# Two-layer attention and expert kernel: queries and keys turned by DMA, GpSimd's split ahead of its value step, and a third PSUM bank for the first score pass

## What is computed

```
q = (x @ Wq.T + bq).reshape(B, L, H, hd); k, v likewise
q = _apply_rope(q, cos, sin); k = _apply_rope(k, cos, sin)      # layer 0
scores = jnp.einsum('bqhd,bkhd->bhqk', q, k) / np.sqrt(hd)
attn = jax.nn.softmax(scores, axis=-1)
out = jnp.einsum('bhqk,bkhd->bqhd', attn, v).reshape(B, L, D)
x = _layernorm(x + out @ Wo.T + bo)
```

## Time and profile before

| | us |
|---|---|
| median of 3 runs | 602.04 (600.29 to 603.62) |
| profiled execution | 603.38, its span 601.6 |
| attention of layer 0, first scores to last maxima | about 17 to 126 |
| attention of layer 1 | about 252 to 367 |
| ScalarE, VectorE busy in the span | 413.9, 429.6 |

### The profile page before, as it was taken

How to read it: one execution, slowest core, us unless ns; L and a number is a source line. 1 busy time by engine, 2 the same in 40 slices (tenths; PEclk the granted TensorE clock), 3 DMA queues, 4 the chain that set the end, 5 groups by cost and what they waited for, 6 DMA issues and landing times.

```text
span 601.6 us, 16720 instructions
## 1 busy us (share of the span) xinstructions
PE 538.7 (90%) x5262; PEld 388.6 (65%) x5262; DVE 429.6 (71%) x1582; ACT 413.9 (69%) x1104; POOL 344.2 (57%) x471
## 2 busy tenths in 40 slices
PE   9899999999779984799999999979999999999950
PEld 7444444447557973544555444758889999999940
DVE  4979999966765304877989996786887788643276
ACT  2279998882624752538999988417778888999824
POOL 4978888342005782673445544456566777777730
PEclk9979999998999997958999999779999999999975
DMA  7493000002001237007910000112221122111363
GB/s 215 112 322 101 2 1 3 2 2 71 7 1 43 47 40 223 6 1 218 302 46 2 3 2 1 54 39 58 51 52 54 59 62 61 59 58 55 125 186 120
DMA packets 53204, 43.12 MB, mean 72 GB/s; under 512 B 14992, under 2 KB 43424, under 8 KB 52992
## 3 DMA queue, kind: packets, MB, share of 16 engines
q1 hardware_dynamic: 45568, 29.98, 17.3%
q0 software_dynamic: 7264, 11.62, 7.4%
q10 hardware_dynamic: 288, 0.46, 0.2%
HBM read 30.17 MB, written 11.87 MB: 70 GB/s over the span
## 4 chain that ended last, share of the span: by engine, by line
PE 70%; DVE 12%; issue 6%; DMA 5%; ACT 4%; POOL 2%; DVEq 0%; ACTq 0%; POOLq 0%; SPq 0%
PE bank L1329 12%; PE bank L1339 11%; PE bank L928 10%; PE bank L911 7%; PE bank L893 6%; PE bank L945 3%; ACT prob L1477 2%; DMA parts<-augs,idx_s 2%; PE bank L969 2%; DVE W L1965 2%; PE bank L1141 2%; PE bank L1382 1%; PE bank L1161 1%; PE bank L953 1%; PE bank L1200 1%
## 5 line engine op out<-in xcount | busy, mean ns | idle before, releaser
L1792 DVE TENSOR_REDUCE mx<-bank 128x2 f32<-128x512 f32 x256 | 163.1, 686 | 24.7 <-PE bank L893 23.7
L1477 ACT ACTIVATE prob<-bank 128x512 f32<-128x512 f32 x256 | 140.7, 609 | 23.0 <-PE bank L911 19.1
L1666 ACT ACTIVATE queries<-bank,prob 128x128 f32<-128x128 f32 x316 | 90.4, 369 | 19.9 <-PE bank L1329 17.0
L1329 PE MATMUL bank<-keys,prob 128*128 x632 | 85.7, 278 | 0.8 <-issue 0.6
L1339 PE MATMUL bank<-W,queries 128*128 x632 | 84.2, 276 | 0.0
L804 POOL DMA_INDIRECT prob<-xs,idx_g x64 | 61.8, 966 | 33.7 <-DVE idx_g L2176 12.6
L1329 PEld LDWEIGHTS bank<-keys,prob 128*128 128x128 f32 x632 | 76.8, 192 | 3.9 <-issue 2.6
L893 PE MATMUL bank<-keys,queries 32*128 32x256 f16 x512 | 77.0, 285 | 2.6 <-issue 1.7
L1339 PEld LDWEIGHTS bank<-W,queries 128*128 128x128 f32 x632 | 76.7, 192 | 1.8 <-issue 0.7
L928 PE MATMUL bank<-prob,augs 128*32 128x256 f32 x1024 | 77.7, 392 | 0.0
L813 POOL DMA_INDIRECT parts<-augs,idx_s x64 | 63.4, 991 | 21.5 <-issue 9.0
(11 more groups left out here) (292 smaller groups left out, 1045.3 us busy)
## 6 DMA issues: line engine op xcount, KB each, us to landing
W<-in_w SPq DMA_DIRECT2D x48, 256.0 KB, 4.0
sum<-zero SPq DMA_DIRECT2D x3, 1024.0 KB, 9.1
xs<-X SPq DMA_DIRECT2D x2, 768.0 KB, 5.2
prob<-xs,idx_g POOLq DMA_INDIRECT x80, 2.6
XB<-sum SPq DMA_DIRECT2D x1, 1024.0 KB, 4.9
Y<-sum SPq DMA_DIRECT2D x4, 256.0 KB, 5.7
W<-sum SPq DMA_DIRECT2D x4, 256.0 KB, 6.5
parts<-augs,idx_s POOLq DMA_INDIRECT x64, 2.2
```

The source lines that it names most:

```text
L1329: last = nc.tensor.matmul(bank[2 + p % 2][:, P * f:P * f + P], wc[:, p % 4, P * f:P * f + P], xsT2[:, bass.ds(at, 1), :], start=True, stop ...
L1477: nc.scalar.activation(prob[:, v % 8, :, :], st_bank(b, v)[:, :], ACT.Exp, scale=SCALE).then_inc(exp_done, 1)
L1666: last = nc.scalar.activation(hid2[:, p % 4, f, :], bank[2 + p % 2][:, P * f:P * f + P], ACT.Gelu, bias=wc[:, p % 4, WB + f:WB + f + 1])
L1792: nc.vector.tensor_reduce(m_at, bank[S1B[u % 2]][:, :].rearrange("p (j k) -> p j k", j=2), AX.X, ALU.max).then_inc(s1_used, 1)
```

## The change

- **Turning.** For batches 1 to 7 of each layer SyncE turns `aug` by two transposing DMAs (`turn`), one for each half t of 128 tokens, each moving queries and keys at once. They write `qkT`, which has three buffers and lies where `keys` does. TensorE's `query_transposes` and `key_transposes`, VectorE's `q_evac` and ScalarE's `keys_evac` remain for batch 0 of each layer alone. The first product of a batch waits for `turned_in`.
- **A signal for each half.** `aug_ready` is raised after each half of the split; all waits on it count twice.
- **GpSimd's order.** `build_aug` of batch i + 1 comes before `build_vaug` of batch i.
- **Third bank.** Bank 6, which took the turned keys, joins `S1B`. A unit of the first pass waits for the maxima three units back, not two.
- **SyncE's order.** The constants come after batch 1's turn. The expert weights come in groups behind turns: in layer 0 four after batch 2's and four after batch 3's, the zeroing after batch 4's; in layer 1 three after each, from batch 2 on.
- `max_transposes` now waits for the evacuation of batch i + 1's projection, which uses bank M5 too.
- `front_evac` keeps its wait for `vaug_ready`.

```diff
-        S1B, STB, OTB, M5, M6, M7 = (0, 1), (2, 3), 4, 5, 6, 7
+        S1B, STB, OTB, M5, M6, M7 = (0, 1, 6), (2, 3), 4, 5, 6, 7
...
+            def turn(lay, b):
+
+                g = b + NB * lay
+                if b > 2:
+                    sp.wait_ge(st_done, 16 * (g - 2))
+                wait_for(sp, turned_in, 32 * (g - 1 - lay))
+                for t in range(2):
+                    sp.wait_ge(aug_ready, 2 * g + t + 1)
+                    sp.dma_start_transpose(qkT[b % 3][:, t, :, :], aug[b % 2][:, t, :, :].rearrange("p h x -> p (h x)")
+                                           ).then_inc(turned_in, 16)
+
+            def batches_in(lay):
+
+                at = ((0, 0, 4, 8, 8, 8, 8, 8), (0, 0, 3, 6, 9, 12, 15, 16))[lay]
+                for b in range(1, NB):
+                    turn(lay, b)
...
             def pool_iteration(lay, i, par):
 
-                build_vaug(lay, i, par)
                 if i < NB - 1:
                     build_aug(pool, lay, i + 1, 1 - par)
+                build_vaug(lay, i, par)
...
+                if i > 0 and u == 0:
+                    pe.wait_ge(turned_in, 32 * (g - lay))
...
+                if g > 0 or u > 2:
+                    pe.wait_ge(s1_used, 16 * g + u - 2)
...
-                    if u == 13 and front_on:
-                        query_transposes(lay, i + 1, nxt)
...
-                    if u == 15 and front_on:
-                        key_transposes(lay, i + 1, nxt)
```

More of the change, by code:

```diff
@@ L145, in program @@
         queries = sb("queries", [P, 4 * NF * P])
-        QT = [queries[:, 512 * i:512 * i + 512].bitcast(F16).rearrange("p (j l) -> p j l", j=NJ) for i in range(2)]
         keys = sb("keys", [P, RING * P])
-        keyT = [keys[:, 512 * i:512 * i + 512].bitcast(F16).rearrange("p (j l) -> p j l", j=NJ) for i in range(2)]
+        qkT = [keys[:, 1024 * i:1024 * i + 1024].bitcast(F16).rearrange("p (t c l) -> p t c l", t=2, l=P) for i in range(3)]
         QT2 = sb("QT2", [P, NJ, L], F16)
@@ L270, in program @@
         proj_done = sem("proj_done")
+        turned_in = sem("turned_in")
         qkv_ready = sem("qkv_ready")
@@ L397, in st_bank @@
         def st_bank(b, v):
-            return bank[(STB + S1B)[v % 4] if last_batch(b) else STB[v % 2]]
+            return bank[(STB + S1B[0:2])[v % 4] if last_batch(b) else STB[v % 2]]
         def last_batch(b):
@@ L1155, in query_transposes @@
                 g = b + NB * lay
-                pe.wait_ge(aug_ready, g + 1)
-                if not (isinstance(b, int) and b in (0, NB - 1)):
-                    pe.wait_ge(qkv_ready, 2 * g + 4)
+                pe.wait_ge(aug_ready, 2 * g + 2)
                 for j in range(NJ):
                     for t in range(2):
-                        last = nc.tensor.transpose(half[M5][:, L * j + P * t:L * j + P * t + P],
+                        last = nc.tensor.transpose(half[M5][:, P * (4 * t + j):P * (4 * t + j) + P],
                                                    aug[par][:, t, 4 * j:4 * j + 4, :], ident_h[:, :])
@@ L1166, in key_transposes @@
                 g = b + NB * lay
-                pe.wait_ge(aug_ready, g + 1)
-                if not (isinstance(b, int) and b == 0):
-                    pe.wait_ge(kt_ready, 2 * g)
+                pe.wait_ge(aug_ready, 2 * g + 2)
                 for j in range(NJ):
                     for t in range(2):
-                        last = nc.tensor.transpose(half[M6][:, L * j + P * t:L * j + P * t + P],
+                        last = nc.tensor.transpose(half[M6][:, P * (4 * t + j):P * (4 * t + j) + P],
                                                    aug[par][:, t, H + 4 * j:H + 4 * j + 4, :], ident_h[:, :])
@@ L1566, in keys_evac @@
                 g = b + NB * lay
-                act.wait_ge(tk_done, g + 1)
-                if not (isinstance(b, int) and g < 2):
-                    act.wait_ge(st_done, 16 * (g - 2) + 8 * pair + 8)
-                nc.scalar.copy(keyT[par][:, 2 * pair:2 * pair + 2, :],
-                               half[M6][:, 2 * L * pair:2 * L * pair + 2 * L]).then_inc(kt_ready, 1)
+                act.wait_ge(tk_done, lay + 1)
+                at = slice(NJ + 2 * pair, NJ + 2 * pair + 2)
+                turned = half[M6].rearrange("p (t j l) -> p t j l", t=2, l=P)
+                nc.scalar.copy(qkT[b % 3][:, :, at, :], turned[:, :, 2 * pair:2 * pair + 2, :]).then_inc(kt_ready, 1)
             def front_evac(lay, b, par, t):
```

88 lines of the change are left out of this document (42 added, 46 removed).

## The result

| | before | after |
|---|---|---|
| median | 602.83 (4 runs, 600.29 to 607.03) | 624.95 (4 runs, 622.62 to 625.34) |
| ratio | | 1.035 (95% interval 1.029 to 1.042) |
| profiled execution, span | 603.38, 601.6 | 622.62, 620.7 |

A forecast was written before the change was run, and what follows sets the result against it. Prediction: VectorE's maxima bound attention batches; the later value step would stall ScalarE's copy. From the profiled 603.4, +8.8 by the chain and +7.8 by clock falls give 620.0 (618.6 against the median); forecast 618 us, range 605 to 631.

The forecast's parts named there:

- The chain: Attention: later value step delays ScalarE's projection copy and the ninth maximum; batch gains and losses together +8.8 us.
- T: End of VectorE's step writing the negated maxima, once per attention batch; 14.24 us apart in layer 0, 14.36 in layer 1.
- Layer 0, batches 2 to 5: Layer 0 attention: each of four batches 1.7 us longer behind the late evacuation, 6.8 us lost.
- Batch 1 of layer 0: Layer 0 attention, partly at half clock already: loses about 1.2 us.
- The clock: TensorE's pause before the second projection halves its clock: six falls at 1.3 us, +7.8, between 0 and +20.
- 4 us for a landing: SyncE's transposing DMAs between split and attention: landing taken as 4 us, room about 8 us, so hidden at no cost.
- (1): TensorE's pause in attention brings the clock down seldom or never; only the chain counts: 611 us, chance 0.25.
- (2): ScalarE's evacuation does not wait for the value step in the end; 15.4 us gained over 14 batches: 587 us, chance 0.10.
- (3): Transposing DMAs land late, at 9.1 us, delaying batches 2 to 7 of each layer: some 30 us, 632, chance 0.12.
- VectorE is the bound: Attention before the change: VectorE's sixteen maxima and small steps set the batch's pace, as long as TensorE feeds it.
- The term of the removal: Attention, 14 of 16 batches: dropping VectorE's 0.69 us copy gains about 0.6 us a batch.
- the third bank (0.5): First score pass: TensorE a tile further ahead removes at most VectorE's 1.1 us idle a batch; half counted.

The follow-up runs named there:

- second series: Later runs beside the kernel before, including the changed kernel unedited (687.8 us) and the changed kernel with 30 matmuls in TensorE's pause (681.8 us).
- the empty matmuls: Changed kernel plus 30 empty matmuls in TensorE's pause before the second half's projection; 1.015 and 1.016 to the kernel before.
- the second profile: Profile of the changed kernel run again without an edit, in a later series; median 687.8 us, 1.025 to the kernel before.

## Why the prediction was right, and where its steps were off

**The chain.** Forecast 618 us, 605 to 631; measured 625. The sign, the place and the mechanism of the loss were right: a value step moved back, a copy that waits for it, and a pause on TensorE and VectorE behind it. Value step T + 7.71 forecast, T + 7.79 measured; evacuation T + 7.76 and 7.87; next T at 15.9 and 16.02. Layer 1: evacuation T + 7.2 and 7.42, next T at 15.4 and 15.57. Batches 6 and 7 gained 0.9 and 0.3 each layer, as forecast.

**The sum.** Its terms against the beats:

- Layer 0, batches 2 to 5: 4 x 1.7 forecast, 4 x 1.77 measured without the clock. Layer 1: 4 x 1.0 and 4 x 1.21.
- Batch 1 of layer 0: 1.2 forecast, 1.47 measured. The first transposing pair was late there, which I had called hidden with all the others: 2.98 us on TensorE.
- Batch 0 of layer 0: a gain of 0.6 forecast; the first beat comes 0.1 later. In the other executions it varied between 25.7 and 27.5 us from the start.
- Batches 0 and 1 of layer 1: -0.2 forecast. Batch 1 is 0.26 shorter; in the 1.4 us between the layers batch 0 is contained, with the experts' stages. These and the 1.3 us behind the last beat no step of mine held. The kernel with the third value buffer, run twice, had 142.0 and 145.4 us between the layers, so I put neither down to the change; it wasn't tested.
- The clock: six falls at 1.3 us, 7.8, forecast; five in this profile, at 1.1, some 5.4. By the median of the second series the falls that the empty matmuls take away cost 6.0. The upper bound of 2.6 us for one was summed wrong: up to 9 us of work in place of 5, less 0.9 hidden, is 3.1, and a fall of the second profile did cost 3.4.

Together: 7.4 in layer 0 and 3.4 in layer 1 by the chain, 5.4 by the clock, 2.8 elsewhere, 19.0 of the 19.1 us. The forecast for the profiled execution was 16.6, as 8.8 by the chain and 7.8 by the clock. The chain was forecast too low: 0.07 us in each of layer 0's four stalled beats, 0.21 in each of layer 1's, 0.3 in batch 1, and the gain of batch 0 that did not come. The clock was forecast too high, by 2.4. That these two nearly cancel is luck; the 2.8 elsewhere are what is left. By the medians the change costs 22.1 and not 19.1 us, and for these 3 us more there is no trace.

**The first landing.** The pairs of the changed kernel: SyncE's queue, TensorE, and the tile's own account (durations in ns of an issue; us to landing):

```profile
21.96 4.15 SPq L611 DMA_TRANSPOSE keys<-augs  x2
```

```profile
28.80 0.61 PE L918 MATMUL bank<-keys 32*128 32x256 f16 x4 [2.98 <-DMA keys<-augs]
```

```profile
L611 SPq DMA_TRANSPOSE keys<-augs x28: 1231/1304/2746, 22.0 to 367.0; - x28
...
DMA to landing us min/median/max: 2.7/2.8/5.4
```

I had 4 us for a landing, from the split's end, with 8 us of room. The median is 2.8, and the first issue stands before it, so that a pair takes 4.1 us as a rule, 5.3 at batch 7 with the value step first, and 6.8 at the beginning of attention. In a stalled beat of 16 us that is hidden, as forecast. In the beats of 12.5 to 13.5 us that the kernel can reach it has 1 to 2 us of room left, and with the value step first, which puts the split off by 1.3 us, under 1 us or none.

**The rivals.** (1) is out: falls come, and fill work takes them away. (2) is out: the value step is what ScalarE waits for, in every batch from 1 to 5 of both layers and for 1.5 us or more in each. (3) is out as priced: no beat waits for the landing but that of layer 0's batch 1. The Trainium skill's figure for the DMA crossbar (VectorE: DVE Perf Modes, "The three transpose paths", 1309 ns for a 128x128 transpose), taken one block after the other, had meant 21 us a pair by my estimate; the trace has eight blocks landing in 2.8 us. The Trainium skill's other page (Advanced Engine Details and Errata, "X-Bar Transpose (TRN2)") has transposing DMAs as fast as others. The trace agrees for the landing, as the 256 KB loads of weights take 3.8 us; the issue on SyncE is longer, 1.3 us against 0.43.

**The steps that failed outright** stand in the account of the kernel before and in a rival. "VectorE is the bound" was wrong: TensorE, with 0.19 us of waiting in the batch shown, set the pace of the steady batches, and VectorE waited for it. The forecast did not suffer, since in the changed kernel both stand still behind ScalarE's copy. But the rival that rests on it did: 14 x 1.1 = 15.4 us for the change without its order. By the medians it is 4 us in the experiment with the value step first, and 11 to 14 with the third value buffer; by the beats it is nothing there, and 7 to 8 us here. The term of the removal (0.6) measured 0.53 and that of the third bank (0.5) 0.25. With three banks and the wait gone, TensorE waits for 0.19 us between 82 and 97 us, by the modelled ends; it stands in the way of the rest.

## What to carry to other kernels

Before a step is moved back on its engine, look up who writes over what it reads: here a copy on another engine had 1.3 us of room, and the step it waits for was moved back behind 4.8 us of work; a third buffer of 1 KB a partition turned 3% of loss into 2% of gain. When a beat grows in an experiment, look at the clock of that very batch before its parts are priced; two of these kernels would have been misread by over 1 us a batch, and how long a fall lasts matters as much as whether there is one. And a gain that hangs on a transfer being hidden has to be worked out at the shorter beat, since that is when its room goes.

## What the hardware showed that I had not expected

- A transposing DMA of 256 KB keeps SyncE busy for 1.3 us at its issue, three times as long as most ordinary ones (0.43 us). The two issues of layer 0's first pair took 2.7 to 4.2 us together.
- A pause of TensorE of 2.5 us in layer 0, and of 1.8 us in layer 1, is followed by a fall of its granted clock in some batches and not in others, in the same kernel. With 0.7 to 0.8 us of the pause left no batch of layer 0 from 2 to 5 has one, in two profiles. Falls last 3.4 us as a rule, and 6.8 or over 10 us in some batches; the cause of that was not looked for.
- The same kernels took 63 to 72 us more in the later series. In the changed kernel, the one with two traces, 64 us of it lie in the stages behind layer 1's attention, and the undisturbed beats of attention were the same to 0.04 us.
